# Self-attention of a perceiver kernel on one core: router rows, norm statistics and one projection half issued earlier

## The chip, the cores and the metric

The kernel runs on one core of one Trainium2 chip. The metric is the device time of one execution in microseconds (us), the median of several runs; lower is better. The engines are TensorE (PE in the profile), VectorE (DVE), ScalarE (ACT), GpSimd (POOL) and SyncE (SP, which here only issues DMAs). Each engine runs its own instructions strictly in the order in which the program issued them; between engines, semaphores order the work. An instruction that waits therefore holds up everything behind it on its own engine.

## The reference, cut to what matters

The model has two layers of cross attention, self attention and a feed-forward part. The change touches the second layer's self attention and the router in front of its experts. There `x` is (4 batches, 128 tokens, 512), the context length is 128, and there are 16 heads of 64:

```python
x = x + L1_xattn(layernorm(x), ctx, ctx, mask, ...)       # ends just before the change
# self attention, per batch b
y = layernorm(x)                       # (x - mean) / sqrt(var + 1e-5)
q, k, v = y @ wq.T, y @ wk.T, y @ wv.T # 512 -> 1024 each
q, k = rotary(q), rotary(k)
p = softmax(mask_causal(q @ k.T * 0.125))
x = x + (p @ v) @ wo.T
# router of the experts, per batch b
y = layernorm(x)
s = softmax(y @ gate_w.T)              # 8 experts
top_scores, sel = top_k(s, 2)
```

The router's rows of a batch depend only on that batch's residual after self attention, so they can be computed while the next batch attends.

## The kernel before, in words

A batch's 128 tokens are the 128 partitions. `X` (128, 4, 512) holds the residual of the four batches.

**The norm.** `norm_rate(b)` (lines 127 to 136) is three DVE instructions (statistics, aggregate, add epsilon) and one square root on ACT. `norm_rows(b)` (138 to 143) is two on DVE, a reciprocal and the normalised rows into `YN[b % 2]`; its reciprocal waits for ACT's square root. `norm_turn(b, ..)` (145 to 159) is four PE transposes into a PSUM bank and an ACT copy into `YT`.

**Cross attention just before.** Its loop ends at line 1230. The last product with `WO1` of batch 3 is still outstanding then; `project_out` (1146) issues it, and DVE adds it to `X[:, 3]`. `phase()` (1251) then makes every engine wait for everything issued so far on PE, ACT, DVE and POOL. After it come a memset on POOL, some DMAs on SP, and the start of self attention (1514).

**Projections.** `project(b, w)` (1301) is a generator of two halves; each half is 8 matmuls into bank 0 (first half) or bank 1 (second), read out by DVE: one copy for V, three rotary multiplications for Q and K, whose sum POOL forms.

**Attention of a batch.** `attend(b, fill)` (1417) is one written-out order: turn Q (8 transposes, ACT copies `QT`), turn K (ACT and DVE copy `KT`), scores in two groups of 16 matmuls, causal mask and row maxima on DVE (16 small instructions, line 1448), 16 exponentials on ACT (1460), turn of the probabilities (16 transposes through banks 2 and 3, line 1350, ACT and DVE copy `P2` in turns), the product with V (32 matmuls, 1475), DVE's scaling (1480), turn of the output (8 transposes, two ACT copies), and the product with `WO2` (1491), which DVE adds to `X` (1494). All turns share banks 2 and 3, and a transpose waits until its bank was read out.

Between these parts stand calls of `fill()`, each of which issues one projection half as work for PE while it would wait: V of this batch, then Q and K of the next, six halves in batches 0 to 2 and two in batch 3. There are six calls: in batch 0 the first is ahead of turn Q, in later ones behind turn K; the others are behind the scores' maxima, behind the exponentials, behind the turn of the probabilities, behind the product with V, and behind the turn of the output.

**The router.** `route(b)` (1359) is a generator of five steps: 1 norm statistics and rows; 2 the transposes (`norm_turn`, into bank `b % 2`) and the DMA of the rows to memory; 3 the gate's 8 small matmuls into bank 7 (1372) and two small DVE instructions; 4 an exponential on ACT, the small softmax, its DMA and the top-2 comparisons on DVE; 5 the token counts (small PE matmuls at 1407, two small DVE instructions). `route_step()` issues the next one. `route(b)` is created at the end of `attend_all(b)` and its steps run inside `attend(b + 1)`: step 1 behind the exponentials, a `fill()`, step 2, then one step each behind the three fills that follow. Batch 3's router runs after attention, in one piece. In batch 0 there is no router to step.

Square root and exponential need different tables on ACT; the trace shows the loads as instructions of their own.

Of the kernel before, what the change touches and what calls it, by code (L numbers as in the profile page):

```python
# [23 lines left out]
class Plan:  # L24
# [25 lines left out]
    def need(self, eng, *toks):  # L50
        for t in toks:
            if t is None:
                continue
            if isinstance(t, list):
                self.need(eng, *t)
                continue
            if self.seen.get((eng, t[0]), 0) < t[1]:
                self.eng[eng].wait_ge(self.sems[t[0]], t[1])
                self.seen[(eng, t[0])] = t[1]
# [5 lines left out]
def build(nc, I, out, D, stop=99):  # L65
    ctx = ExitStack()
    with ctx:
# [70 lines left out]
        def norm_rows(b, t):  # L138
            need("dve", t)
            t = tick("dve", dve.reciprocal(SM[:, 8 + b:9 + b], SM[:, 4 + b:5 + b]))  # L140
            need("dve", t, st["yn"][b % 2])
            return tick("dve", dve.tensor_scalar(YN[:, b % 2, :], X[:, b, :], MV[:, b, 0:1], SM[:, 8 + b:9 + b],
                                                 ALU.subtract, ALU.mult))
# [17 lines left out]
        def layernorm(b, bk=None):  # L161

            return norm_turn(b, norm_rows(b, norm_rate(b)), b % 2 if bk is None else bk)
# [387 lines left out]
        t_yt = [None] * 4  # L551
# [397 lines left out]
        t_yt = layernorm_all(bg)  # L949
# [240 lines left out]
        def load_next():  # L1190
            name, dst, src = next_loads.pop(0)
            t_wb[name] = dma("sp", name, dst, src)
# [19 lines left out]
        for g in range(256 + 2):  # L1212
            if g < 256:
                turn_piece(g)
                if g % 8 == 0:
                    pair_sums(g // 8)
                score_chunk(g + 12)
                exp_chunk(g + 8)
            if g >= 2:
                project_out(g - 2)  # L1220
                if g % 8 == 2:
                    bg(1)
                value_piece(g - 2)
            if g % 8 != 2:
                bg(1)
            if g < 42 and g % 3 == 0:
                bg(1)
            if bgen[0] is None and g > 200 and g % 5 == 0:
                need("sp", *bgs["free"], *kv_done[3])
                load_next()  # L1230
        while waiting:
            project_out(300)
        while next_loads:
# [106 lines left out]
        def turn(dst, src, blocks, t_src, t_dst_free, engs):  # L1340

            nonlocal tr_n
            need("pe", t_src)
            t_last = []
            for j0 in range(0, blocks, 4):
                bk = 2 + tr_n % 2
                tr_n += 1
                need("pe", free[bk])
                for j in range(4):
                    m = pe.transpose(bank[bk][:, 128 * j:128 * j + 128], src(j0 + j), IDN[:])  # L1350
                t = t_pe = tick("pe", m)
                e = engs[(j0 // 4) % len(engs)]
                need(e, t, t_dst_free)
                t = free[bk] = tick(e, (dve.tensor_copy if e == "dve" else act.copy)(dst(j0), bank[bk][:].rearrange("p (a b) -> p a b", a=4)))
                t_last.append(t)
            return t_last, t_pe
# [63 lines left out]
        def attend(b, fill):  # L1420

            nonlocal t_sc, t_avb, t_wo
            s = b % 2
            if b == 0:
                fill()
            tq, qr_free[s] = turn(lambda j: QT2[:, j:j + 4, :], lambda j: QR[:, s, 128 * j:128 * j + 128], 8,
                                  t_qr[b], t_sc, ["act"])
            tk, kr_free[s] = turn(lambda j: KT2[:, j:j + 4, :], lambda j: KR[:, s, 128 * j:128 * j + 128], 8,
                                  t_kr[b], t_sc, ["act", "dve"])
            if b > 0:  # L1430
                fill()
            need("pe", *tq, *tk)
            for quad in range(2):
                need("pe", free[4 + quad], free[6 + quad])
                t_half = [None, None]
                for hh in range(4 * quad, 4 * quad + 4):
                    for half in range(2):
                        r = slice(64 * half, 64 * half + 64)
                        m = pe.matmul(bank[4 + 2 * half + quad][:, 128 * (hh % 4):128 * (hh % 4) + 128],
                                      QT2[r, hh, :], KT2[r, hh, :], start=True, stop=True)  # L1440
                        if hh % 4 == 3:
                            t_half[half] = t_sc = tick("pe", m)
                for half in range(2):
                    bk = 4 + 2 * half + quad
                    need("dve", t_half[half], t_avb)
                    for q in range(4):
                        h = 2 * (4 * quad + q) + half
                        t = tick("dve", dve.tensor_tensor_reduce(
                            T2[:, h, :], bank[bk][:, 128 * q:128 * q + 128], CM[:], 1.0, NEG,
                            ALU.add, ALU.max, M2[:, 0, h:h + 1]))  # L1450
                    free[bk] = t
            need("dve", t)
            t = tick("dve", dve.tensor_scalar(M2[:, 1, :], M2[:, 0, :], -0.125, None, ALU.mult))
            fill()
            if b == 3:
                for q in range(4, 10):
                    load_group(q, *yt_readers)
            need("act", t)
            for h in range(16):
                t = tick("act", act.activation(T2[:, h, :], T2[:, h, :], ACT.Exp, bias=M2[:, 1, h:h + 1], scale=0.125,  # L1460
                                               accum_out=M2[:, 2, h:h + 1]))
            route_step()
            fill()
            route_step()
            tp, t_avb = turn(lambda j: P2[:, j:j + 4, :], lambda j: T2[:, j, :], 16, t, None, ["act", "dve"])
            need("dve", t)
            t_rs = tick("dve", dve.reciprocal(M2[:, 3, :], M2[:, 2, :]))
            fill()
            route_step()
            need("pe", t_vv[b], *tp)  # L1470
            for h in range(16):
                bk = 4 + h // 8
                if h % 8 == 0:
                    need("pe", free[bk])
                m = pe.matmul(bank[bk][:, 64 * (h % 8):64 * (h % 8) + 64], P2[:, h, :], VV[:, s, 64 * h:64 * h + 64],
                              start=True, stop=True)
            vv_free[s] = t = tick("pe", m)
            need("dve", t, t_rs)
            for n in range(2):
                t = free[4 + n] = tick("dve", dve.tensor_tensor(  # L1480
                    O2[:, 512 * n:512 * n + 512].rearrange("p (h d) -> p h d", h=8),
                    bank[4 + n][:].rearrange("p (h d) -> p h d", h=8),
                    M2[:, 3, 8 * n:8 * n + 8].unsqueeze(2).broadcast_to([128, 8, 64]), ALU.mult))
            fill()
            route_step()
            to, _ = turn(lambda j: OT2[:, j:j + 4, :], lambda j: O2[:, 128 * j:128 * j + 128], 8, t, t_wo, ["act"])
            fill()
            route_step()
            need("pe", *to, free[6], t_wb["ldb3"])
            for j in range(8):  # L1490
                m = pe.matmul(bank[6][:], OT2[:, j, :], WO2[:, j, :], start=(j == 0), stop=(j == 7))
            t_wo = tick("pe", m)
            need("dve", t_wo)
            x_tok[b] = free[6] = tick("dve", dve.tensor_tensor(X[:, b, :], X[:, b, :], bank[6][:], ALU.add))
# [7 lines left out]
        def route_step():  # L1502
            if routing[0] is not None:
                next(routing[0], None)

        def attend_all(b):
            units = itertools.chain(project(b, 2), *(project(b + 1, w) for w in range(2) if b < 3))
            attend(b, lambda: next(units, None))
            rest(units)
            if routing[0] is not None:  # L1510
                rest(routing[0])
            routing[0] = route(b)

        t_yt[0] = layernorm(0, 6)
        t_n = [None] + [norm_rows(1, norm_rate(1))] + [None] * 2
        rest(project(0, 0))
        t_yt[1] = norm_turn(1, t_n[1], 7)
        t_n[2] = norm_rows(2, norm_rate(2))
        rest(project(0, 1))
        t_n[3] = norm_rows(3, norm_rate(3))  # L1520
        t_yt[2] = norm_turn(2, t_n[2], 6)
        t_yt[3] = norm_turn(3, t_n[3], 7)
        for b in range(4):
# [595 lines left out]
```

How the kernel before makes its waits and increments, by code:

```python
    def need(self, eng, *toks):  # L50
        for t in toks:
            if t is None:
                continue
            if isinstance(t, list):
                self.need(eng, *t)
                continue
            if self.seen.get((eng, t[0]), 0) < t[1]:
                self.eng[eng].wait_ge(self.sems[t[0]], t[1])
                self.seen[(eng, t[0])] = t[1]
# [5 lines left out]
def build(nc, I, out, D, stop=99):  # L65
# [1941 lines left out]
                                if inc is not None:  # L2007
                                    ins.then_inc(*inc)
                        with E[eng].Else():
                            for o in own:
                                if own[o] == eng:
                                    E[eng].drain().then_inc(P.sems[o], by[o])
                        E[eng].end_ifs()
                if eng in ("pool", "dve"):
                    for o in own:
                        if own[o] != eng:
                            E[eng].wait_ge(P.sems[o], P.count[o])
                if eng == "pool":
                    for i in range(4):
                        pool.indirect_dma_start(LB[i][:], None, YD, bass.IndirectOffsetOnAxis(
                            ap=FIN[:, i:i + 1], axis=0)).then_inc(P.sem_of("xlb"), 16)
                if eng == "dve":
                    dve.wait_ge(P.sem_of("xlb"), 64)
            E[eng].end_ifs()
        for i in range(4):
            t = tick("hb", pool.indirect_dma_start(
```

## Time and profile before

| | us |
|---|---|
| median of 3 runs (1935.92, 1936.03, 1937.83) | 1936.03 |
| profiled execution, whole | 1930.54 |
| its span in the trace | 1929.2 |
| PE busy | 1762.4 (91%) |
| DVE busy | 1248.4 (65%) |
| ACT busy | 948.7 (49%) |
| POOL busy | 443.3 (23%) |

All times of the trace are counted from the start of the span. Self attention with its router lies between about 1340 and 1560 us: the entry up to 1367, then batch 0 up to 1410, batch 1 up to 1459, batch 2 up to 1505.6, batch 3 up to 1548.5, and the router of batch 3. Busy time is an average over stages; for this change only the stretches inside this window matter. In a timeline row the columns are start, duration, engine, line, operation, output and inputs, count of instructions merged, and in brackets how long the engine sat idle before and what released it.

### The profile page before, as it was taken

To read this page: it belongs to the slowest core of one execution; us is meant where nothing else is said; L and a number is where in the kernel's file an instruction comes from. 1 tells how busy PE (TensorE), PEld (TensorE's weight loads), DVE (VectorE), ACT (ScalarE), POOL (GpSimd) and SP (SyncE) were. 2 spreads that over 40 slices of the span, in tenths; PEclk is the share of its full clock that TensorE was granted. 3 is DMA by queue.
4 is the path that set the end of the run, shared out by engine and by line. 5 is a ranking of instruction groups with operands and counts; after the bars stand their busy time and mean duration, and the time that the engine had idled before them with its cause. 6 is when DMAs were issued, how large, how long until landed. Compare 5 with 4: busy or idle time off the path is not lost.

```text
span 1929.2 us, 25864 instructions
## 1 busy us (share of the span) xinstructions
PE 1762.4 (91%) x9438; PEld 1438.9 (75%) x9438; DVE 1248.4 (65%) x2521; ACT 948.7 (49%) x1969; POOL 443.3 (23%) x262
## 2 busy tenths in 40 slices
PE   6889999997999889999999999998888869889896
PEld 4667787875878679999899988886455547768785
DVE  5888989884543426667677767996434356665753
ACT  4454545452243225556566656885222345565552
POOL 1444546451000012113111211221111012221221
PEclk9999999998999999999999999999999879999998
DMA  6122222113720399778677767676300346685721
GB/s 232 66 87 88 88 88 88 69 63 131 270 75 1 104 283 318 234 231 244 195 237 221 239 193 201 183 222 225 131 6 6 121 152 231 239 286 187 259 75 61
DMA packets 147134, 310.03 MB, mean 161 GB/s; under 512 B 11472, under 2 KB 100816, under 8 KB 135440
## 3 DMA queue, kind: packets, MB, share of 16 engines
q1 hardware_dynamic: 145072, 301.85, 47.7%
q0 software_dynamic: 1920, 6.36, 1.0%
q8 instruction: 81, 1.33, 0.3%
q14 instruction: 61, 0.50, 0.1%
HBM read 226.88 MB, written 81.28 MB: 160 GB/s over the span
## 4 chain that ended last, share of the span: by engine, by line
PE 68%; DVE 21%; ACT 5%; DMA 3%; issue 2%; DVEq 0%; POOL 0%; ACTq 0%; SPq 0%; POOLq 0%
PE bank L101 11%; PE bank L102 10%; PE bank L103 10%; PE bank L1089 4%; PE bank L1629 4%; PE bank L1630 4%; PE bank L1633 4%; PE bank L1311 3%; DVE PTL L1096 2%; PE bank L1044 2%; DVE TT L1046 2%; PE bank L1115 2%; PE bank L1116 2%; DVE CNL L426 2%; DVE FA L340 2%
## 5 line engine op out<-in xcount | busy, mean ns | idle before, releaser
L1096 DVE TENSOR_TENSOR PTL<-bank,PTH 128x512 fp32r<-128x512 f32 x256 | 176.0, 688 | 95.0 <-ACT PTH L1094 93.6
L1094 ACT CAST PTH<-bank 128x512 fp32r<-128x512 f32 x256 | 149.9, 586 | 165.1 <-PE bank L1089 165.1
L1616 DVE TENSOR_TENSOR WS<-EW,WS 128x1024 fp32r<-128x1024 f32 (+1 forms) x120 | 150.5, 1264 | 70.8 <-ACT WS L1613 70.4
L1074 ACT ACTIVATE TT<-TT,MX 128x512 f32<-128x512 f32 x256 | 186.5, 729 | 8.6 <-DVE MX L1064 8.6
L1046 DVE CUSTOM_DVE_ANT_0 TT<-bank,MASK 128x512 f32<-128x512 f32 x256 | 174.3, 682 | 8.7 <-POOL MASK L1027 6.6
L1613 ACT CAST WS<-EW 128x1024 fp32r<-128x1024 f32 (+1 forms) x144 | 139.3, 977 | 48.6 <-PE bank L1633 44.2
L1089 PE MATMUL bank<-IDN,TT 128*128 128x128 f32 x1024 | 155.2, 274 | 4.0 <-DVE RS L1139 2.9
L101 PE MATMUL bank<-BCH,WKT 128*128 128x256 f32 x512 | 149.7, 292 | 4.8 <-DVE BCL L608 4.1
L102 PE MATMUL bank<-BCL,WKT 128*128 128x256 f32 x512 | 146.0, 285 | 0.0
L103 PE MATMUL bank<-BCH,WKT 128*128 128x256 f32 x512 | 146.0, 285 | 0.0
L466 POOL TENSOR_TENSOR KS<-KS,FH 128x512 f32<-128x512 f32 x60 | 100.7, 1678 | 197.2 <-DVE FL L456 197.1
L1115 PE MATMUL bank<-PTH,VG 128*128 128x256 f32 x512 | 142.6, 300 | 0.2 <-DVE PTL L1096 0.2
L1002 POOL CAST VG<-VR 128x1024 fp32r<-128x1024 f32 x32 | 33.2, 1038 | 448.6 <-DMA VR<-tmp_v 387.7
L1089 PEld LDWEIGHTS bank<-IDN,TT 128*128 128x128 f32 x1024 | 118.8, 140 | 21.2 <-issue 5.6
L1116 PE MATMUL bank<-PTL,VG 128*128 128x256 f32 x512 | 133.3, 282 | 0.0
L101 PE MATMUL bank<-FH,CNH 128*128 128x512 f32 x256 | 104.9, 410 | 25.7 <-DVE S L356 16.9
L1629 PE MATMUL bank<-WS,XG 128*128 128x512 f32 (+1 forms) x288 | 111.8, 388 | 12.0 <-DVE HH L1716 9.7
L101 PE MATMUL bank<-WKH,CTH 128*128 128x512 f32 x256 | 105.5, 412 | 14.6 <-DVE CTL L295 10.1
L1630 PE MATMUL bank<-WS,XG 128*128 128x512 f32 (+1 forms) x288 | 108.2, 376 | 0.0
L1116 PEld LDWEIGHTS bank<-PTL,VG 128*128 128x128 f32 x512 | 97.3, 190 | 11.9 <-issue 3.4
L101 PEld LDWEIGHTS bank<-BCH,WKT 128*128 128x128 f32 x512 | 99.2, 194 | 7.7 <-DVE BCL L608 4.7
L103 PE MATMUL bank<-FH,CNL 128*128 128x512 f32 x256 | 103.2, 403 | 0.0
(291 smaller groups left out, 4598.4 us busy)
## 6 DMA issues: line engine op xcount, KB each, us to landing
EW<-in_ewg SPq DMA_DIRECT2D x48, 1024.0 KB, 5.3
KST<-tmp_k SPq DMA_DIRECT2D x43, 768.0 KB, 5.8
tmp_k<-EKH SPq DMA_DIRECT2D x128, 256.0 KB, 2.8
EW<-in_ewg SPq DMA_DIRECT2D x24, 768.0 KB, 4.2
CT<-in_ctxT SPq DMA_DIRECT2D x32, 512.0 KB, 4.4
CN<-in_ctxN SPq DMA_DIRECT2D x32, 512.0 KB, 3.4
BCT<-in_ctxT SPq DMA_DIRECT2D x32, 512.0 KB, 3.4
tmp_k<-EKL SPq DMA_DIRECT2D x64, 256.0 KB, 2.9
```

What stands on the lines that cost most here:

```text
L101: pe.matmul(o, ah, bh, start=start, stop=False, skip_group_check=skip)
L102: pe.matmul(o, ah, bl, start=False, stop=False, skip_group_check=skip)
L103: return pe.matmul(o, al, bh, start=False, stop=stop, skip_group_check=skip)
L1046: t2 = free[bk] = tick("dve", dve.tensor_tensor_reduce(TT[:, sl, 512 * kc:512 * kc + 512], bank[bk][:], MASK[:, b % 2, 512 * kc:512 * kc + ...
L1074: t_e[(n, kc)] = tick("act", act.activation(TT[:, sl, cs], TT[:, sl, cs], ACT.Exp, bias=MX[:, n % 4, 5:6], scale=SC1, accum_out=SUM[:, b % ...
L1089: m = pe.transpose(bank[bk][:, 128 * j:128 * j + 128], TT[:, n % 4, 128 * kt:128 * kt + 128], IDN[:])
L1096: t = free[bk] = tick("dve", dve.tensor_tensor(PTL[:, q], bank[bk][:], f(PTH[:, q]), ALU.subtract))
L1115: pe.matmul(bank[vb][:, 0:256], v, PTH[:, q, js], start=(kt == 0), stop=False)
L1116: m = pe.matmul(bank[vb][:, 0:256], v, PTL[:, q, js], start=False, stop=(kt == 15))
L1616: t_lo = tick(low, E[low].tensor_tensor(WS[:, s, 1, 0:n * w], src, f(WS[:, s, 0, 0:n * w]), ALU.subtract))
L1629: pe.matmul(o, a[j][0], WS[:, s, 0, j * w:j * w + w], start=start and j == 0, stop=False)
L1630: pe.matmul(o, a[j][1], WS[:, s, 0, j * w:j * w + w], start=False, stop=False)
```

## The change

Four edits, all in the order of issue; no instruction is added or removed.

1. The statistics of batches 0 to 2 (`norm_rate`) are issued before the outstanding product of cross attention and before `phase()`.
2. At the start of self attention the rows of batches 0 and 1 are normalised first, then batch 0 is turned, then the statistics of batch 3 are issued; the rows of batches 2 and 3 are both normalised between the two projections of batch 0.
3. In `attend`, the router's steps move one place forward: step 1 (statistics and rows) is issued at the end of `attend_all`, right behind the addition to `X`; step 2 behind turn K and the first fill, ahead of the scores; no step stands between the exponentials and the fill behind them; step 3 comes behind that fill, step 4 behind the next, step 5 behind the next, and the last call finds the generator exhausted.
4. In batch 0 there is a second `fill()` behind the exponentials; the last fill of that batch then finds no half left.

```diff
@@ -1228,6 +1228,7 @@
                 load_next()
+        t_rate = [norm_rate(b) for b in range(3)]
         while waiting:
             project_out(300)
@@ -1429,6 +1430,7 @@ attend
             if b > 0:
                 fill()
+            route_step()
             need("pe", *tq, *tk)
@@ -1459,9 +1461,10 @@
             for h in range(16):
                 t = tick("act", act.activation(T2[:, h, :], T2[:, h, :], ACT.Exp, bias=M2[:, 1, h:h + 1], scale=0.125,
                                                accum_out=M2[:, 2, h:h + 1]))
-            route_step()
             fill()
             route_step()
+            if b == 0:
+                fill()
             tp, t_avb = turn(...)
@@ -1510,14 +1513,16 @@ attend_all
             routing[0] = route(b)
-
-        t_yt[0] = layernorm(0, 6)
-        t_n = [None] + [norm_rows(1, norm_rate(1))] + [None] * 2
+            route_step()
+
+        t_n = [norm_rows(b, t_rate[b]) for b in range(2)] + [None] * 2
+        t_yt[0] = norm_turn(0, t_n[0], 6)
+        t_rate.append(norm_rate(3))
         rest(project(0, 0))
         t_yt[1] = norm_turn(1, t_n[1], 7)
-        t_n[2] = norm_rows(2, norm_rate(2))
+        for b in range(2, 4):
+            t_n[b] = norm_rows(b, t_rate[b])
         rest(project(0, 1))
-        t_n[3] = norm_rows(3, norm_rate(3))
         t_yt[2] = norm_turn(2, t_n[2], 6)
         t_yt[3] = norm_turn(3, t_n[3], 7)
```

## Rows read from the trace of the kernel before

**Rows 1.** The page, part 4: share of the span in the chain that ended last
```profile
PE 68%; DVE 21%; ACT 5%; DMA 3%; issue 2%; DVEq 0%; POOL 0%; ACTq 0%; SPq 0%; POOLq 0%
```

**Rows 2.** Timeline, entry of self attention: start, duration, engine, line, operation [idle before]
```profile
1337.90 0.61 DVE L1127 TENSOR_TENSOR YT<-bank,YT 64x128 f32<-64x128 f32 x2 [1.13 <-ACT YT L1123]
...
1339.73 0.69 DVE L1175 TENSOR_TENSOR X<-X,bank 128x512 f32<-128x512 f32 x1 [1.22 <-PE bank L1171]
...
1343.18 0.16 DVE L140 RECIPROCAL SM<-SM 128x1 f32<-128x1 f32 x1 [1.63 <-ACT SM L136]
...
1343.84 0.69 DVE L130 BATCH_NORM_STATS2 BNS<-X 128x6 f32<-128x512 f32 x1
1344.07 1.08 PE L149 MATMUL bank<-IDN,YN 128*128 128x128 f32 x4 [4.38 <-DVE YN L142]
...
1344.77 0.15 DVE L134 TENSOR_SCALAR SM<-MV 128x1 f32<-128x1 f32 x1
```

**Rows 3.** Timeline, the turns of batches 2 and 3 at the entry
```profile
1362.95 0.60 PE L149 MATMUL bank<-IDN,YN 128*128 128x128 f32 x4
...
1366.58 0.66 PE L149 MATMUL bank<-IDN,YN 128*128 128x128 f32 x4 [3.03 <-DVE YN L142]
```

**Rows 4.** Timeline, batch 0 from the turn of the probabilities on
```profile
1385.01 3.30 PE L1350 MATMUL bank<-IDN,T 128*128 128x128 f32 x16 [2.07 <-ACT T L1460]
...
1388.10 4.12 PE L1311 MATMUL bank<-WA,YT 128*128 128x512 f32 x8
...
1392.06 3.68 PE L1475 MATMUL bank<-VV,P 128*128 128x64 f32 x32
...
1399.06 1.04 PE L1350 MATMUL bank<-IDN,O 128*128 128x128 f32 x8
...
1399.70 1.07 ACT L1354 COPY OT<-bank 128x512 f32<-128x512 f32 x2 [11.63 <-PE bank L1350]
...
1399.94 3.60 PE L1311 MATMUL bank<-WA,YT 128*128 128x512 f32 x8
```

**Rows 5.** Timeline, batch 0's addition and the turns of batch 1
```profile
1410.44 0.69 DVE L1494 TENSOR_TENSOR X<-X,bank 128x512 f32<-128x512 f32 x1 [5.51 <-PE bank L1491]
...
1410.88 1.07 ACT L1354 COPY QT<-bank 128x512 f32<-128x512 f32 x2 [10.10 <-PE bank L1350]
...
1411.61 1.06 PE L1350 MATMUL bank<-IDN,KR 128*128 128x128 f32 x8 [0.33 <-ACT QT L1354]
...
1416.14 0.69 DVE L1316 COPY VV<-bank 128x512 f32<-128x512 f32 x1 [2.75 <-PE bank L1311]
```

**Rows 6.** Timeline, batch 1 behind its exponentials
```profile
1427.22 1.28 ACT L136 ACT_TABLE_LOAD   x1
...
1430.90 1.08 PE L149 MATMUL bank<-IDN,YN 128*128 128x128 f32 x4 [5.75 <-DVE RT L1327]
...
1431.78 3.81 PE L1350 MATMUL bank<-IDN,T 128*128 128x128 f32 x16
...
1440.40 3.77 PE L1475 MATMUL bank<-VV,P 128*128 128x64 f32 x32
```

**Rows 7.** Timeline, the same place in batch 2 (batch 3 repeats it)
```profile
1476.02 1.28 ACT L136 ACT_TABLE_LOAD   x1
...
1479.26 2.52 PE L1350 MATMUL bank<-IDN,T 128*128 128x128 f32 x12
```

**Rows 8.** Timeline, the end of batch 3
```profile
1539.31 1.28 ACT L136 ACT_TABLE_LOAD   x1
...
1539.90 8.52 PE L1491 MATMUL bank<-WO,OT 128*128 128x512 f32 x16
...
1550.32 0.20 ACT L136 ACTIVATE SM<-SM 128x1 f32<-128x1 f32 x1 [9.72 <-DVE SM L134]
```

**Rows 9.** Windows: stretch, length, busy us (count) per engine, granted PE clock, DMA share, GB/s
```profile
1364.00:1366.00 2.00, 0.00 (x0) 0.00 (x0) 1.63 (x7) 0.45 (x2) 1.26 (x1) 1.00 1.04 424
...
1386.00:1388.00 2.00, 1.99 (x10) 1.61 (x9) 0.69 (x1) 0.80 (x2) 0.00 (x0) 0.50 0.00 0
```

## The prediction

> **What bounds the kernel now.** I read the page's chain of waits first: TensorE carries 68% of it, DVE 21% and ACT 5% [rows 1]. So an edit of order pays only where TensorE stands still, and the brackets of the timeline say where that is. I then read the timeline through self attention, looking only at TensorE rows with a bracket. Six waits touch the edits. At the entry TensorE waits 4.38 us for the first normalised rows [rows 2], and 3.03 us for the rows of batch 3 [rows 3]. In batch 0 it waits 2.07 us for the exponentials [rows 4]. In batches 1 to 3 it waits for the router's rows of the batch before: 5.75 us in batch 1 [rows 6]. The reason is a queue. The router's square root stands behind 16 exponentials on ACT and needs a table load of 1.28 us that can start only when they are done (1427.22); DVE then makes the rows, and TensorE's transposes for them stand in front of the turn of the probabilities, which itself needs only the exponentials. In batch 1 the transposes also use bank 0, which the fill's rotary instructions, queued behind DVE's wait, have still to read; the releaser named is that rotary line [rows 6].
>
> **The sum.** All durations are of the profiled execution: 1930.54 us, of which 1929.2 is the span. The median of the runs is 1936.03, 5.5 above it; I take the saving worked out on the trace from the median.
>
> *Entry, first rows.* DVE is free at 1337.90 + 0.61 = 1338.51. One set of statistics takes 1344.77 + 0.15 - 1343.84 = 1.08 us [rows 2]; three take 3.24 and end at 1341.75. The addition to batch 3's residual, which TensorE would have ready for 1339.73, now queues behind them: 2.02 us late, and every engine waits for it in `phase()`. It ends at 1342.44. ACT's three square roots and the table load are done by then. From the reciprocal to the first transpose is 1344.07 - 1343.18 = 0.89 [rows 2], so the transposes start at about 1342.47 + 0.89 = 1343.36 against 1344.07. Gain 0.7. SP's weight loads and POOL's memset start some 2 us later too; nothing reads them for a long time. Bounds: if the sets overlapped fully with the matmul the addition would move less, gain 1.5; if each took 0.25 more through waits on its own results, gain 0.
>
> *Entry, rows of batch 3.* Their statistics now run in DVE's idle time during the first projection and the rows before the second. The turn of batch 3 follows that of batch 2 at once: 3.03 gained [rows 3]. What is next late is nothing: ACT and POOL have finished K of batch 0 before turn K asks for it. I take 3.0.
>
> *Batch 0, third half in the softmax.* The 2.07 of waiting is filled. The following half took 4.12 where a later one takes 3.60, because the granted clock was 0.50 there [rows 4, 9]; without the gap I expect 3.60, gain 0.5. The price is at the end of the batch: no half is left behind the turn of the output, so the product with `WO2` waits for the copies. Turn starts 1399.06, copies end 1399.70 + 1.07 = 1400.77, the next half started at 1399.94: new wait 0.8 [rows 4]. Net 2.07 + 0.5 - 0.8 = 1.8. Bounds: 1.1 (the slower half stays, and the rotary multiplications delay DVE's share of the probability copies by 0.2) and 2.0.
>
> *Batches 1 to 3, softmax.* The turn of the probabilities can start when the last exponential ends, which is where the table load now starts. In batch 1 it starts 1431.78 - 1427.22 = 4.56 later [rows 6], in batch 2 1479.26 - 1476.02 = 3.24 later [rows 7], in batch 3 as in batch 2. Removed: 4.56 + 2 x 3.24 = 11.0. The gate's matmuls of step 3 now stand where TensorE waits anyway.
>
> *Batches 1 to 3, entry.* This is what it costs. ACT's square root now stands in front of the copies of `QT`. It waits for the addition (starts 1410.44, 0.69 + 0.03), a set of statistics (1.08) and starts about 0.05 after, at 1412.29; the copy follows at 1412.40, where it stood at 1410.88 [rows 5]. Turn K waits on that copy (its bracket, 0.33, names it [rows 5]), so TensorE stands still 1.5 us longer, three times: -4.5. The table load itself I cost at nothing: at the end of batch 3 the same instruction's load ran at 1539.31 while ACT idled 9.72 us before the root [rows 8]; without that cover it adds 1.28 each time. Next, step 2's transposes come ahead of the scores: about 0.5 each (0.60 busy for four, rows 3, less the overlap with what follows): -1.5. Where they use bank 0 (batches 1 and 3) they must wait for DVE's copy of V's first half, which is in the same bank and runs 0.69 after the matmuls [rows 5]: with the handovers 0.75, twice: -1.5.
>
> *Behind the softmax.* In batch 1, turn, half and gate took 1440.40 - 1431.78 = 8.62 [rows 6]; batch 0, without gate and with a shorter wait before it, took 1392.06 - 1385.01 = 7.05 [rows 4]. Gain 1.6. In batch 2 the clock rose sooner and I count nothing (0 to 0.5); in batch 3 the gate was hidden by a copy. Step 4's comparisons, now ahead of DVE's scaling of the output, need DVE there; the half that TensorE works on meanwhile gives them 3.60 us before anyone asks for the scaled output, so I cost them at nothing (if they took longer, the excess would be a wait before the turn of the output). In batch 3 the small matmuls of step 5 stood between ACT's last copy, which ended where the load starts (1539.31), and the product at 1539.90 [rows 8]; now they stand in a wait ahead: gain 0.55.
>
> Batches 1 to 3 together: 11.0 - 4.5 - 1.5 - 1.5 + 1.6 + 0.55 = 5.7. Everything: 0.7 + 3.0 + 1.8 + 5.7 = 11.2. The one thing that the trace before doesn't show is TensorE's clock after the new 1.9 us waits at the entry of batches 1 to 3. From one side: 3.03 us of waiting passed at a granted clock of 1.00 [rows 9], cost 0. From the other: behind 2.07 us in batch 0 it went to 0.50 and the half took 0.52 longer [rows 4, 9]; three times 1.6. I take 0.7, nearer to the first. Forecast: 11.2 - 0.7 = 10.5 saved, 1925.5 us.
>
> **A rule against it.** In rows, 0.50 is the lower of the two clock levels, 1.2 GHz, and 1.00 is 2.4 GHz; both followed waits [rows 9]. The Trainium skill, page "TensorE: Matmul & The Clock Gate", Part 1, says that the array falls to half rate when TensorE has been idle and comes back only after it has been busy for a while. By that rule alone every new wait would be followed by a slow stretch; the trace agrees for batch 0 and does not for the entry. What it would do here is the third rival.
>
> **Rivals.**
> 1. *The table load isn't hidden.* If the load waits with the root it stands in front of `QT`'s copies: 3 x 1.28 = 3.8 less, 1929.3. For it: in batches 1 to 3 the load came directly before the root. Against: the row at 1539.31, with the same form of wait [rows 8].
> 2. *DVE's queue becomes the bound.* Step 4 and the rotary instructions meet the copies of the probabilities and the scaling; 1 us in each of four batches and the first-rows gain gone: 4.7 less, 1930.2. For it: DVE is second in the chain [rows 1]. Against: each has a half of 3.60 beside it.
> 3. *The clock* (the other side, slower). If after each entry wait TensorE stays at the lower level until the scores are through, turn K, V's first half and the transposes run at half speed: a half costs up to 3.6 more, turn K up to 1.1 (rows 5), the transposes 0.5 (1.08 against 0.60, rows 2, 3). 5.2 us, three times, is 15.6: 1936.0 - 11.2 + 15.6 = 1940.4. The change stops paying once more than 11.2 / 15.6, some 70%, of these stretches is slow. Against: 3.03 us of waiting left the clock at 1.00, and the half after batch 0's wait was slow for only 0.52.
> 4. *The saving is given back* in the expert stage, if its weights arrive too late to start sooner: 1936.0. Against: those loads are issued inside attention and move forward with it.
>
> **How the numbers follow.** Forecast 0.76, with its own range 1922.5 to 1928.5 (bounds of the terms above, not all on one side); rival 1 0.08, rival 2 0.07, rival 3 0.04, rival 4 0.05. About 0.2% (3.9 us) is what a measurement tells from no change. Faster by more: the forecast, rival 1 and about half of rival 2, 0.88. Within: the other half and rival 4, 0.08. Slower: 0.04. The range 1922 to 1930 leaves out rivals 3 and 4, the upper part of 2 and a little below.
>
> **What would show it.** The profile of the changed kernel should have: the addition L1175 near 1341.8 and the first L149 near 1343.4; no wait in front of the fourth L149 at the entry; no bracket on TensorE before batch 0's turn of the probabilities and one of about 0.8 before its L1491; in batches 1 to 3 a wait of about 1.9 before turn K, released by ACT, the load of L136 early, and before batch 1's turn of the probabilities at most 2.1 instead of 5.75 (TensorE ran dry at 1430.90 - 5.75 = 1425.15, the exponentials end at 1427.22), less what the gate fills. It is wrong if the wait before turn K is near 3 (the load), if the clock in those stretches is 0.50, or if the turn of the probabilities is not released by the exponentials.

## The result and the profile after

The changed kernel took 1922.9 us (median of 6 runs, 1917.8 to 1928.4); the kernel before, in the same comparison, 1936.4 (6 runs, 1935.8 to 1941.9). The ratio is 0.9923, 95% interval 0.9901 to 0.9946: 14.9 us faster, between 10 and 19. The forecast was 10.5 faster and 1925.5. The median lies inside the range of 1922 to 1930; the ratio, laid on 1936.03, gives 1921.1, just below it. A second comparison gave 0.9936 (0.9911 to 0.9960). The 12 runs of the two have a mean span of 1922.5, the 49 runs of the kernel before in three later comparisons one of 1935.1: 12.6 less, each mean good to about 1 us. Single executions of either kernel differ by 10 us and more, so below I use traces for lengths and means of runs for times.

The profiled execution after had a span of 1926.0 (before 1929.2). In it, self attention from the last DVE instruction of line 1127 to batch 3's addition took 1540.46 - 1340.27 = 200.2 us against 1548.46 - 1337.90 = 210.6: 10.4 less. The stages ahead were 2.4 longer and the expert stage behind 4.8 longer in that execution, which is why its span fell by only 3.2.

The timeline of the entry, changed kernel (columns as in [rows 2]):

```profile
1340.27 0.61 DVE L1127 TENSOR_TENSOR YT<-bank,YT 64x128 f32<-64x128 f32 x2 [1.13 <-ACT YT L1123]
1340.91 0.70 DVE L130 BATCH_NORM_STATS2 BNS<-X 128x6 f32<-128x512 f32 x1
...
1343.87 0.15 DVE L134 TENSOR_SCALAR SM<-MV 128x1 f32<-128x1 f32 x1
1344.05 0.69 DVE L1175 TENSOR_TENSOR X<-X,bank 128x512 f32<-128x512 f32 x1
...
1344.83 0.17 DVE L140 RECIPROCAL SM<-SM 128x1 f32<-128x1 f32 x1
1344.94 0.95 POOL L1289 MEMSET ZERO<- 128x1024 f32 x1 [23.07 <-DVE X L1175]
1345.03 1.15 DVE L142 TENSOR_SCALAR YN<-X,MV,SM 128x512 f32<-128x512 f32 x1
...
1346.32 1.08 PE L149 MATMUL bank<-IDN,YN 128*128 128x128 f32 x4 [4.27 <-DVE SM L140]
...
1365.33 1.04 PE L149 MATMUL bank<-IDN,YN 128*128 128x128 f32 x8
```

The three sets of statistics stand ahead of the addition, as forecast, and the first transpose starts 6.05 us after line 1127's last instruction, where it was 6.17 [rows 2]. The turns of batches 2 and 3 are now one run of eight transposes with no wait; the 3.03 of [rows 3] is gone.

TensorE's timeline around batch 1, changed kernel; batch 0's half behind the turn of the probabilities and its product with `WO2` stand first:

```profile
1388.03 3.60 PE L1312 MATMUL bank<-WA,YT 128*128 128x512 f32 x8
...
1400.29 7.10 PE L1494 MATMUL bank<-WO,OT 128*128 128x512 f32 x16 [0.77 <-ACT OT L1355]
1407.23 1.04 PE L1351 MATMUL bank<-IDN,QR 128*128 128x128 f32 x8
...
1410.10 1.06 PE L1351 MATMUL bank<-IDN,KR 128*128 128x128 f32 x8 [1.84 <-ACT QT L1355]
...
1415.48 0.63 PE L149 MATMUL bank<-IDN,YN 128*128 128x128 f32 x4 [0.88 <-DVE VV L1317]
1416.04 2.06 PE L1441 MATMUL bank<-KT,QT 64*128 64x128 f32 x32
...
1424.99 0.95 PE L1373 MATMUL bank<-GAT,YT 128*128 128x8 f32 x8
1427.25 1.09 PE L1351 MATMUL bank<-IDN,T 128*128 128x128 f32 x8 [1.31 <-ACT T L1462]
```

Read the brackets: 0.77 before `WO2` (forecast 0.8), 1.84 before turn K where [rows 5] had 0.33 (1.5 forecast, 1.51 found), 0.88 before the router's transposes in bank 0 (0.75), and before the turn of the probabilities 1.31, released by the exponentials, instead of 5.75 [rows 6]. The half at 1388.03 takes 3.60 instead of 4.12 [rows 4]. The table load of the moved root ran early, while ACT was idle, as in [rows 8]:

```profile
1400.20 1.28 ACT L136 ACT_TABLE_LOAD   x1
...
1409.28 0.20 ACT L136 ACTIVATE SM<-SM 128x1 f32<-128x1 f32 x1 [7.79 <-DVE SM L134]
1409.39 1.06 ACT L1355 COPY QT<-bank 128x512 f32<-128x512 f32 x2
```

### The profile page after: what moved, and what is told of

Same layout as the page of the kernel before. It is cut to its first block and busy times, and to the rows that moved or that the text cites. A ratio compares the mean times of both kernels' runs of the same rounds, so it can differ in the third digit from the quotient of the medians.

```text
span 1926.0 us, 25868 instructions
## 1 busy us (share of the span) xinstructions
PE 1762.4 (92%) x9438; PEld 1438.0 (75%) x9438; DVE 1250.9 (65%) x2521; ACT 948.2 (49%) x1969; POOL 442.9 (23%) x262
## 5 line engine op out<-in xcount | busy, mean ns | idle before, releaser
L102 PE MATMUL bank<-FL,CNH 128*128 128x512 f32 x256 | 103.5, 404 | 0.0
```

Of the source, the lines that this page charges most:

```text
L102: pe.matmul(o, ah, bl, start=False, stop=False, skip_group_check=skip)
```

## The experiments

Three theories were set against each other. A: the order alone makes the saving, and what lies beyond it is chance in the expert stage. B: the surplus comes from the stages ahead of the change, or the parts don't add. C, formed after the first four runs: part of the saving is TensorE's granted clock, which falls behind the long waits and comes back late. The rows of windows below have the columns of [rows 9]; the third number from the end is the mean granted clock. Time at the lower of the two levels is summed over stretches of 2 us, each as length x (1 - clock) x 2.

**The whole change again.**

> The changed kernel once more, unaltered. Its self attention (from the last DVE instruction of line 1127 to the addition of batch 3) took 200.2 us against 210.6 before, 10.4 less, but its six runs lay between 1917.8 and 1928.4 with a median of 1922.9. Theory A (the saving is made in self attention; the rest is the expert stage, whose length varies from execution to execution with how its gathers meet its weight loads): self attention again 200.2 within 0.3, and the expert stage (from that addition to the end) other than the 385.5 of the first trace by some us. Theory B (the rest comes from the stages ahead of the change): the difference lies before line 1127's last instruction, expert stage within 1 us of 385.5.

Ratio 0.9936, runs 1918.0 to 1927.7. Self attention was not the same. The windows over it, first trace and second:

```profile
1340.27:1540.46 200.19, 175.03 (x738) 102.31 (x738) 82.61 (x293) 57.63 (x182) 21.19 (x17) 0.92 0.20 78
```

```profile
1336.80:1532.90 196.10, 170.36 (x738) 98.36 (x738) 82.61 (x292) 57.64 (x182) 21.20 (x17) 0.95 0.21 79
```

DVE's, ACT's and POOL's busy times agree within 0.01; TensorE's is 4.7 less, and the clock is 0.95 instead of 0.92. The second trace had 20.4 us at the lower level, the first 30.7: 4.1 us of length for 10.3 at the lower level, 0.40 per us. So A's "again 200.2 within 0.3" is wrong, and its expert stage (383.8 against 385.5) is not where the executions differ most. B falls as well: the stages ahead differ by 3.4, not by the whole.

**The parts, each alone.** Entry only:

```diff
+        t_rate = [norm_rate(b) for b in range(3)]   # ahead of project_out, and edit 2
```

> Only edits 1 and 2 (statistics and rows at the entry). Theory A: from line 1127's last instruction to batch 0's scores 32.7 us as in the whole change, against 35.9 before; nearly all of the 3.2 from the wait of 3.03 before batch 3's turn, next to nothing from the first rows; whole time 3.2 less than before, give or take the expert stage. Theory B (parts don't add, the expert stage shifts with its start): the time differs from that by more than 3 us and does so in every run.

Ratio 0.9968 (0.9952 to 0.9984), 5.5 us in the mean span (12 runs, 1930.3 against the 23 runs beside it, 1935.8). Its trace has a stretch up to batch 0's addition of 69.3 us against 72.5 before: 3.3, as A says. B's "by more than 3 us" doesn't hold here.

Half only:

```diff
             fill()
+            if b == 0:
+                fill()
             route_step()
```

> Only edit 4 (the second fill behind batch 0's exponentials). Theory A: batch 0 from its scores to batch 1's turn Q 34.3 us against 36.4, 2.1 less; whole time 2.1 less. Theory B: another time by more than 3 us in every run.

Ratio 0.9994 (0.9978 to 1.0011), mean 1935.9: nothing to be seen in the time. Yet batch 0 did what it should. TensorE's timeline in it:

```profile
1376.81 2.06 PE L1439 MATMUL bank<-KT,QT 64*128 64x128 f32 x32 [0.88 <-DVE KT L1354]
...
1411.10 1.04 PE L1350 MATMUL bank<-IDN,QR 128*128 128x128 f32 x8
```

That is 34.29 us; before it was 1410.24 - 1373.82 = 36.42. The interval holds 2.1 us as well as none. The window over this trace's self attention shows what hid it there, 216.1 us long with 58 us at the lower level:

```profile
1340.89:1557.02 216.13, 184.50 (x738) 109.11 (x738) 81.19 (x293) 58.24 (x182) 21.17 (x17) 0.87 0.19 72
```

Router only:

```diff
+            route_step()          # behind turn K and its fill, and at the end of attend_all
-            route_step()          # behind the exponentials
```

> Only edit 3 (the router's steps one place forward). Theory A: batches 1 to 3 take 45.8, 44.9 and 42.5 us against 48.8, 46.5 and 42.9, 5.0 less; whole time 5.0 less. Sum of the three parts: 10.3. Theory B: another time by more than 3 us in every run.

Ratio 0.9937 (0.9913 to 0.9960), mean 1925.1, 10.7 us less than before: twice the 5.0, so A's time is missed. Its batches took 44.2, 44.8 and 41.3 against A's 45.8, 44.9 and 42.5. TensorE around batch 1's softmax has the brackets of the whole change (1.31) and no slow half behind it:

```profile
1434.71 1.09 PE L1350 MATMUL bank<-IDN,T 128*128 128x128 f32 x8 [1.31 <-ACT T L1461]
1436.05 1.20 PE L1350 MATMUL bank<-IDN,T 128*128 128x128 f32 x8 [0.24 <-ACT P L1354]
1437.09 3.60 PE L1311 MATMUL bank<-WA,YT 128*128 128x512 f32 x8
```

Before, the same turn took 3.81 [rows 6], and the half behind it 4.37:

```profile
1435.38 4.37 PE L1311 MATMUL bank<-WA,YT 128*128 128x512 f32 x8
```

The means of the three parts, 5.5, 0 and 10.7, sum to 16.2, against 12.6 to 13.3 for the whole; with about 1 us of doubt on each that neither proves nor refutes that they add.

The runs taken together say more. In the 49 runs of the kernel before, a higher mean granted clock goes with a shorter span: about 1.4 us per 0.001, correlation -0.84; the other unfilled kernels give 1.5 to 1.7. The mean clock was 0.9624 in the 23 runs of the kernel before, 0.9635 with the entry alone, 0.9611 with the half alone and 0.9668 with the router alone. Priced at 1.5 us per 0.001, the clock makes 1.6, -2.0 and 6.6 us of the three savings, and leaves 4.0, 2.0 and 4.2 for the order, where A had 3.2, 2.1 and 5.0. That is an estimate with about 1 us of doubt on each; it accounts for the missing 2.1 of the half and for most of what the router's part saved beyond its 5.0.

**The clock by itself.** Four kernels put matmuls that nobody reads into TensorE's waits ahead of the turn of the probabilities. They add work and move nothing:

```diff
+        def spin(n):
+            need("pe", free[6], free[7], t_wb["ldb3"])
+            for j in range(n):
+                m = pe.matmul(bank[6][:], IDN[:], WO2[:, j % 8, :], start=True, stop=True)
...
+            spin((4, 10, 8, 14)[b])      # behind the exponentials' fill
```

> The kernel before, its order unchanged, with matmuls whose result nobody reads (IDN times a slice of WO2 into bank 6) put into TensorE's waits behind the exponentials: 4, 10, 8 and 14 of them in batches 0 to 3, each 0.43 us at full clock, fewer than the waits hold. Theory C (clock): what the router edit saved beyond its 5.0 us (10.7 in the mean of its runs) is TensorE's clock, which falls to the lower level behind the long waits; then this kernel keeps the clock at 1.00 through the turns of the probabilities and the halves behind them and is 3 to 6 us faster than before, with a mean granted clock 0.002 to 0.004 higher. Theory A (only the order counts; the rest is chance in the expert stage): no change, 0 within 1 us, or slower by the energy of it.

Ratio 1.0008 (0.9993 to 1.0024). One such matmul shows in the trace as two passes of 0.43, 0.86 together, so 30.9 us of them went into waits of 20.0. The kernel lost nothing by it that the interval shows (means 1935.1 against 1934.2), with a mean granted clock of 0.968 against 0.963: an estimate of 10 us came back from the clock. The size was my mistake, and the next but one mends it. The same in the changed kernel:

> The changed kernel with such matmuls in the waits that are left before the turn of the probabilities: none, 2, 2 and 9 in batches 0 to 3. Theory C: batch 3, where the wait is near 5 us, keeps its clock through the turn, the product with V (5.0 us against 3.5 in the other batches) and WO2 (8.5 against 7.0): 2 to 4 us faster than the changed kernel (some 1919 to 1921 in the median). Theory A: as the changed kernel, 1923 to 1926.

Ratio 0.9925 (0.9910 to 0.9941), mean 1920.1: 2.4 less than the changed kernel's 1922.5, inside C's 2 to 4, but with about 1.4 us of doubt on the difference; the median, 1921.6, lies between C's band and A's. It was also overfilled by 3.7. In its trace batch 3's product with V took 3.76, as C said, but `WO2` 8.72, so there C failed.

```diff
-            spin((4, 10, 8, 14)[b])
+            spin((2, 6, 4, 8)[b])
```

> The kernel before with fewer of the matmuls that nobody reads: 2, 6, 4 and 8 behind the exponentials of batches 0 to 3. One of them proved to be two passes and takes 0.86 us, so they fill 1.7, 5.2, 3.5 and 6.9 of the waits of 2.07, 5.75, 4.39 and 7.83 and delay nothing. Theory C (clock): before_spin had put in 30.9 us of such work where the waits hold 20.0, and was no slower in the mean (1935.1 against 1934.2); what the clock gave back is therefore near 10 us, and this kernel is 5 to 9 us faster than before, mean granted clock 0.968 against 0.963. Theory A: as before.

Ratio 0.9940 (0.9926 to 0.9953), mean 1923.4 against 1935.1: 11.7 us faster than the kernel before, with the same order of all its work and 40 more passes on TensorE. That is more than C's 5 to 9, and A's "as before" is out. TensorE behind the exponentials of batch 1, in this kernel:

```profile
1424.12 5.31 PE L1424 MATMUL bank<-WO,IDN 128*128 128x512 f32 x12
1430.04 0.63 PE L149 MATMUL bank<-IDN,YN 128*128 128x128 f32 x4 [0.60 <-DVE RT L1327]
...
1432.81 3.60 PE L1311 MATMUL bank<-WA,YT 128*128 128x512 f32 x8
```

The transposes still wait for the same rotary instruction, but take 0.63 instead of 1.08, and the half 3.60. The windows 1430 to 1438, first of the kernel before, then of this one (granted clock third from the end):

```profile
1430.00:1434.00 4.00, 3.10 (x15) 2.91 (x16) 1.02 (x4) 1.17 (x2) 1.27 (x1) 0.51 0.17 66
1434.00:1438.00 4.00, 4.00 (x12) 2.32 (x12) 1.27 (x3) 1.87 (x2) 0.00 (x0) 0.63 0.00 0
```

```profile
1430.00:1434.00 4.00, 3.67 (x23) 2.78 (x24) 1.54 (x3) 2.54 (x4) 1.24 (x1) 1.00 0.04 15
1434.00:1438.00 4.00, 4.00 (x23) 2.70 (x21) 1.51 (x5) 0.41 (x1) 0.12 (x1) 1.00 0.01 4
```

> The changed kernel with 0, 1, 1 and 5 such matmuls (0.9, 0.9 and 4.3 us in waits of 1.3, 1.3 and 4.9). Theory C: faster than after_spin (mean span 1920.1), whose matmuls overfilled the waits by 3.7 us: 1917 in the mean, the gain over the changed kernel (1922.5) smaller than that of before_spin_fit over before, because the change has already taken away most of the long waits. Theory A: 1922.5.

Ratio 0.9915 (0.9901 to 0.9929), mean 1917.7, as C said: 4.8 less than the changed kernel, less than half of what the same filling gave before the change. These two kernels also price the order at the same clock. The windows over self attention, first `before_spin_fit`, then `after_spin_fit`:

```profile
1338.32:1541.46 203.14, 186.62 (x778) 104.67 (x778) 81.23 (x292) 57.99 (x182) 21.21 (x17) 0.96 0.20 76
```

```profile
1333.93:1530.34 196.41, 175.25 (x752) 100.00 (x752) 82.64 (x293) 57.65 (x182) 21.19 (x17) 0.96 0.21 79
```

Both had 17.1 us at the lower level. They lay in the same places: 10.2 us up to batch 0's addition, none in batches 1 and 2, 6.8 in batch 3. So the difference, 6.7 us in the traces and 5.7 (with some 2 us of doubt) in the means of 5 runs each, is not the clock. By stretch it is 4.0 up to batch 0's addition, 1.5 and 1.3 in batches 1 and 2, and nothing (-0.1) in batch 3.

It understates the order a little. In `after_spin_fit` the filling did delay the turn of the probabilities, because its first matmul waited for the read-out of the gate's bank:

```profile
1420.71 1.12 PE L1425 MATMUL bank<-WO,IDN 128*128 128x512 f32 x2 [0.99 <-DVE SCO L1379]
1421.67 1.04 PE L1351 MATMUL bank<-IDN,T 128*128 128x128 f32 x8
```

From the scores to that turn it took 11.86 us in batch 1, against 1427.25 - 1416.04 = 11.21 in the changed kernel; in batches 2 and 3 the delay was 0.6 and 0.2. In `before_spin_fit` none of the four turns came later than before. With these 1.4 us the order is worth about 8 us in the traces and 7 in the means.

**The kernel before again**, unaltered:

> The kernel before, unaltered, for a second trace. Its first trace had a span of 1929.2, while 40 runs of it have a mean of 1935. Theory C: this trace is longer, and the difference lies in time at the lower clock level (48, 41 and 45 us ahead of, in and behind self attention in the first).

Span 1931.8. The window over its self attention, with 47.8 us at the lower level where the first trace had 41.0:

```profile
1333.89:1547.23 213.34, 180.45 (x738) 106.72 (x738) 81.30 (x293) 58.23 (x182) 21.18 (x17) 0.89 0.19 73
```

2.8 us for 6.8, again about 0.4 per us. Ahead of self attention and behind it the times at the lower level were 41 and 48, against 48 and 45: there the two traces even out.

**The entry's price, and the first rows.** The root behind turn K, the transposes in bank 1:

```diff
-            t_y = norm_turn(b, t, b % 2)
+            t_y = norm_turn(b, t, 1)
...
+            route_step()          # step 1, behind turn K
             if b > 0:
                 fill()
             route_step()
...
             routing[0] = route(b)
-            route_step()
```

> The changed kernel with the router's step 1 issued behind turn K (ahead of the fill) instead of at the end of the batch before, and the router's transposes always in bank 1. By the working of the prediction this takes away the wait before turn K (1.84 against 0.33 us) in three batches and the wait of 0.88 for V's copy in two: 4.5 + 1.7 = 6.2 less, self attention 194 where the first trace had 200.2; median 1917 to 1919. If the rows come too late for the transposes behind the fill, 1 to 2 us per batch are given back. Theory C adds that shorter waits there let the clock fall less often.

Ratio 0.9916 (0.9898 to 0.9934), mean 1917.7, self attention 195.0. TensorE in batch 1:

```profile
1402.68 1.07 PE L1351 MATMUL bank<-IDN,KR 128*128 128x128 f32 x8 [0.33 <-ACT QT L1355]
1403.58 3.60 PE L1312 MATMUL bank<-WA,YT 128*128 128x512 f32 x8
1407.02 0.60 PE L149 MATMUL bank<-IDN,YN 128*128 128x128 f32 x4
1407.55 2.06 PE L1442 MATMUL bank<-KT,QT 64*128 64x128 f32 x32
```

Both waits that the change had put there are gone, the rows come in time, and 4.8 us of the 6.2 show in the mean. What C added isn't borne out: the mean granted clock was 0.965 against the changed kernel's 0.966, and 34 us of its self attention lay at the lower level. Its batch 3 ran at the lower level for long (the product with V 7.06 us), which is chance or the wait of 4.74 ahead of it.

```diff
         while waiting:
             project_out(300)
+        t_rate = [norm_rate(b) for b in range(3)]   # moved from ahead of the loop
```

> The changed kernel with the statistics of batches 0 to 2 issued behind the addition to batch 3's residual instead of ahead of it. The addition then stands 1.9 us after line 1127's last instruction instead of 3.8, and the statistics (3.1 us) come after it, so the first transpose should start 6.0 to 6.6 us after it in both: the time doesn't change (0 within 1 us). If issuing them ahead was worth what the prediction gave it (0.7), this kernel is slower by 0.7 to 1.5.

Ratio 0.9941 (0.9919 to 0.9963), mean 1923.5 against 1922.5: not told apart in the time. The trace does tell: the first transpose starts 1347.57 - 1340.31 = 7.26 us after line 1127's last instruction, against 6.05 and above the 6.0 to 6.6 expected; POOL's memset stands beside the rows here too (1.11 us). Issuing the statistics ahead is worth 1.2 against issuing all three behind, and 0.1 against the kernel before, which had only one set in front of the first rows.

**Everything together**: the last but one, with the filling `spin((0, 1, 1, 5)[b])`.

> The best so far (router's step 1 behind turn K, its transposes in bank 1; mean span 1917.7) with the same 0, 1, 1 and 5 matmuls. In its trace batch 3 ran the product with V in 7.06 us and WO2 in 9.03, against 3.5 and 7.0 at full clock. Theory C: those 5 us come back in part, mean span 1912 to 1915. Theory A: 1917.7.

Ratio 0.9869 (0.9849 to 0.9889): median 1912.9, mean 1911.6, some 23 us faster than the kernel before and 11 faster than the changed one, at the near edge of C's 1912 to 1915. Its self attention took 189.6 us. TensorE at the end of batch 3:

```profile
1505.82 4.56 PE L1425 MATMUL bank<-WO,IDN 128*128 128x512 f32 x10 [0.52 <-DVE SCO L1379]
1510.21 1.04 PE L1351 MATMUL bank<-IDN,T 128*128 128x128 f32 x8
...
1513.57 3.76 PE L1488 MATMUL bank<-VV,P 128*128 128x64 f32 x32 [0.88 <-DVE P L1355]
...
1521.44 9.04 PE L1504 MATMUL bank<-WO,OT 128*128 128x512 f32 x16 [0.77 <-ACT OT L1355]
```

The product with V is back at 3.76 from 7.06; `WO2`, behind a sparse stretch, still falls to the lower level (9.04 against 9.03): that part of C's 5 us did not come back.

## What was right in the prediction, and what failed in it

The waits were forecast well; the time, at 1921.1 by the ratio, fell below the stated range because of the clock. Leaving the clock out, the prediction counted 11.2 - 1.6 - 0.5 = 9.1 us for the order, and 1.6 + 0.5 - 0.7 = 1.4 for the clock; found were about 7 to 8 and 5.

*Entry, first rows: wrong by its size.* Forecast 0.7, found 0.1. The addition came 3.78 after line 1127's last instruction (forecast 3.85). What I had not seen is that the rows then run beside POOL's memset: 1.15 us instead of 0.55, which is the whole difference. The trace before had the memset beside statistics, where it cost nothing.

*Entry, batch 3's rows: right.* 3.0 forecast; the whole entry up to batch 0's scores is 32.7 against 35.9 us.

*Batch 0: right in the sum.* 1.8 forecast; 34.3 against 36.4, 2.1. But the clock's part was larger than the 0.5 I gave it: with its wait filled the kernel before took 1391.19 - 1385.38 = 5.81 us from the turn of the probabilities to the product with V, where it had taken 7.05 [rows 4], 1.24 less.

*Batches 1 to 3: right in the waits*, as the brackets above show. Forecast 5.7, less 0.7 for the clock, 5.0; the first trace: 45.84, 44.92 and 42.27 against 48.80, 46.52 and 42.70, 5.0. That the two agree is luck. The 0.7 was for a slower clock behind the new waits, and no trace shows one. What was missing instead is 0.25 in each of the two batches that use bank 0 (from turn K to the scores 1.5 longer, 1.25 forecast), 0.4 behind batch 1's softmax (from the turn of the probabilities to the product with V 7.46 us against 8.62, 1.2 for the forecast 1.6, since the slow half came again), and 0.4 more in batch 3; 0.3 in each of batches 1 and 2, behind the product with V, came on top unforecast. The sum for self attention, 10.5, met the first pair of traces (10.4).

*The clock: the step that failed.* I wrote that the one unknown was "TensorE's clock after the new 1.9 us waits", bounded it by 0 and 1.6 on the side of a loss, and took 0.7 off. I priced the waits that the change adds and let those that it removes go at what one trace showed. The runs showed the opposite sign. Time at the lower level in self attention was 41 and 48 us in two traces before and 31 and 20 in two after; the mean granted clock of the runs went from 0.963 to 0.966. At the 0.4 us per us found in two pairs of traces, 0.0035 x 2 x 1930 = 13.5 us less at the lower level is 5.4 us, and with the order's 7 to 8 from the fitted pair that makes 12.4 to 13.4, against the 12.6 found. The runs of the kernel before say the same: their line of span against clock, read at the changed kernel's mean clock, gives 1930.2, so 4.9 us are the clock and 7.7 the order. So about four tenths of the gain are the clock, where the prediction had it take 0.7 away and give back only the 1.6 and 0.5 below. The step from clock to time is shown by `before_spin_fit`, which changed nothing but the filling of the waits; the split for the change itself is an estimate. My 10.5 agreed with the first traces partly by luck: "gain 1.6" behind batch 1's softmax and 0.5 in batch 0 were already clock, read from a trace in which TensorE happened to be granted more (0.965) than in the kernel's usual run (0.963), and they were counted once each, although a slow stretch behind the softmax can come in any batch.

*The rule against it.* Rival 3 made the new waits of 1.8 us as costly as the old ones. In three traces of kernels with those waits (the whole change twice, the router's part once) the clock never fell behind them. In batches 1 and 2 it still fell behind the wait of 1.31 before the turn of the probabilities: once each in the first trace (0.76 over 1427 to 1431 in batch 1), once in the router's part, never in the second trace of the whole. In batch 3 it fell in all three, behind the wait of 4.74 before that turn (the 16 transposes took 3.63, 3.56 and 3.52 us) and again before `WO2` (8.7 to 9.5 us). So waits of 1.84, and of 3.03 at the entry before, left the clock at 1.00, and one of 1.31 did not always: the length of a wait alone does not tell here which stretch will be slow. The Trainium skill, "TensorE: Matmul & The Clock Gate", Part 1, says that an idle array falls to half rate and needs a busy stretch to come back; the filled waits agree (1.00 instead of 0.51 and 0.63). It does not say that every wait is followed by a slow stretch, as the prediction read it. Its remark that the number of slow matmuls varies from run to run of the same kernel fits the spread of 10 us here.

*Rivals.* 1 is refuted by the load at 1400.20 (and those at 1443.62 and 1488.55 in the next batches). 2: in batches 0 to 2 no wait of TensorE for DVE behind the exponentials was longer than 0.3 us; in batch 3 one was 0.88, in a place where the gate's matmuls had stood before. 4: the saving was not given back, since the means differ by 12.6. The expert stage took 380 to 391 us in the 14 traces; the longest, 390.6, also had the most time at the lower level (61 us, the others 43 to 54), so part of that spread is the clock. The rest, and what the stage does with its start, was not tried and stays open.

## What to carry to other kernels

Price a wait of the matmul engine twice: by its bracket, and by what runs behind it at the lower clock. Where a wait can't be removed, filling it with matmuls that nobody reads was worth 11.7 us here (0.6%), about as much as the whole rewriting of the order. But measure first how long one of them takes and whether it has a wait of its own: filled beyond the waits by 10.9 us, the same trick gained nothing. And when runs of one kernel differ by 10 us, take no saving off a single trace: look at the granted clock of that trace and at the mean of the runs first.

## What the runs showed of the hardware

A normalisation of 128x512 on DVE took 0.55 us alone, 1.11 and 1.15 beside a memset on POOL, and 1.52 beside a tensor-tensor instruction on POOL (changed kernel, 1359.68, line 142). A statistics instruction of the same size took 0.69 us with the memset beside it and without. A table load of 1.28 us ran while ACT was idle and ended 7.8 us before the square root that needed it started. A fill of 12 passes of 0.43 in a wait of 5.75 us kept the granted clock at 1.00 through a sparse turn of 16 transposes behind it, where in the kernel before about 7 us were spent at the lower level.
